# Score groups of three steps in six PSUM banks, one bank for the other work, in a cross-attention kernel

## The chip, the cores and the metric

One NeuronCore of a Trainium2 chip runs the whole program. The metric is device time in microseconds (us) of one execution. The kernel before takes 739.46 us, the median of three executions (738.22 to 741.74).

## The reference

Eight batch elements; 256 queries and 1601 context positions each, width 256, 16 heads of 16.

```python
x = layer_norm(hidden, ln1_w, ln1_b)
q = (x @ q_w + q_b)                       # 8 x 256 x 256, 16 heads of 16
k = (ctx @ k_w + k_b); v = (ctx @ v_w + v_b)     # 8 x 1601 x 256
scores = einsum('bhqd,bhkd->bhqk', q, k) / 4     # masked
out = softmax(scores) @ v                 # 8 x 16 x 256 x 1601 probabilities
hidden = out @ cproj_w + cproj_b + hidden
y = layer_norm(hidden, ln2_w, ln2_b)
return hidden + gelu(y @ fc_w + fc_b) @ proj_w + proj_b      # inner width 1024
```

## The kernel before

The kernel is written engine by engine: each engine has its own instruction list in program order, and semaphores join the lists. Nothing is reordered by a scheduler. What stands ahead of an instruction in its engine's list holds it up.

The work of a batch is cut into 4 slots of 4 heads, and a slot into 13 steps (KT) of 128 context positions; a batch has 52 steps. In a step TensorE (PE) forms the scores of 4 heads (4 matmuls of 64 rows, two at a time, L1140), ScalarE (ACT) takes the exponential of all 1024 columns in one instruction (L596) and writes it to a buffer of `pr`, and PE multiplies it by V (the "value products", L1147, 8 matmul instructions per step, in four column tiles of 32) into the bank `O`.

Between the steps PE does "units", nearly all for the next batch: 8 K units (`k_unit`, a K tile of 384 or 450 columns as a product of three terms), 13 V units (`v_unit`, one tile of 128 positions), the turning of the normalised x (XT), the Q product, the output projection of the batch before (`cproj`), and 8 maxima (`max_unit`, scores of a sample of the keys, from which VectorE takes each query's largest value). VectorE (DVE) empties the bank of every unit. K and Q go to DRAM and come back in the layout of the scores: `store_k`, then `first_fill` (7 DMAs a slot, issued by SP), which a slot's first maximum waits for. The maxima go into rows of `qst` by `first_rows` and are due when the slot's scores begin.

The eight PSUM banks are: `S` 4 banks (two steps of scores), `O` one bank of value products, `KB` (K units and half of the maxima), `MB` (the other half), `XB` (V, XT, Q, output projection).

Two steps make a pair; a batch has 26. PE's list for pair p is: the scores of both steps, each behind a wait for the exponential two steps earlier; the units that the tables `K_AT`, `V_AT`, `MAX_AT` and the rest put at p; the value products of the pair before. Where a slot ends inside a pair (p = 7 and 20) the units stand between its two steps of value products. DVE's list follows the same tables. GpSimd (POOL) splits the context of the batch after next into a high and a low part (L528, L533) as soon as the units that read the old one are done. In the last batch it splits the weights of the closing layers instead (L557 to L561). After the last batch the two layers of the MLP run (`mlp`).

Of the kernel before, what the change touches and what calls it, by code (L numbers as in the profile page):

```python
# [31 lines left out]
F32 = mybir.dt.float32  # L32
# [4 lines left out]
ALU = mybir.AluOpType  # L37
# [22 lines left out]
NKM = max(NKE)  # L60
CHUNK = [c for c in range(CH) for _ in range(NT[c])]
# [38 lines left out]
HEAD_MAX = [(s, j) for s in range(2) for j in range(NJ)]  # L100

# [5 lines left out]
def kb_pairs(b):  # L107

    return sorted([p for p in K_AT if b + 1 < B] + [p for p, (d, _, _) in MAX_AT.items() if b + d < B])


def mb_pairs(b):

    return sorted(p for p, (d, _, _) in MAX_AT.items() if b + d < B)


def xb_pairs(b):

    return sorted(([CPROJ_AT] if b > 0 else []) + ([XT_AT, Q_AT] + list(V_AT) if b + 1 < B else []))


def uses_before(head, pairs, b, p):

    return head + sum(len(pairs(i)) for i in range(b)) + sum(q < p for q in pairs(b))


KB_HEAD = len(HEAD_K) + len(HEAD_MAX)
MB_HEAD = len(HEAD_MAX)
XB_HEAD = KT + 2


def kb_use(b, p):
    return uses_before(KB_HEAD, kb_pairs, b, p)


def mb_use(b, p):
    return uses_before(MB_HEAD, mb_pairs, b, p)


def xb_use(b, p):  # L140
    return uses_before(XB_HEAD, xb_pairs, b, p)


def pair_of(table, what):
    return [p for p, w in table.items() if w == what][0]


XB_END = XB_HEAD + sum(len(xb_pairs(b)) for b in range(B))
MB_END = MB_HEAD + sum(len(mb_pairs(b)) for b in range(B))
KB_END = KB_HEAD + sum(len(kb_pairs(b)) for b in range(B))  # L150
# [1226 lines left out]
```

## Time and profile before

| | us |
|---|---|
| median of 3 executions (lowest, highest) | 739.46 (738.22, 741.74) |
| the profiled execution, its own time | 738.16 |
| its span, first to last instruction | 736.4 |
| PE busy with matmuls | 690.8 (94%) |
| ACT busy | 446.9 (61%) |
| DVE busy | 379.8 (52%) |
| POOL busy | 123.0 (17%) |

The span has four stretches: the head up to the first scores at 56.0 us, seven batches with units for the next one, a last batch without them (574.5 to 632.7 us) and the MLP. The granted clock is 0.991 of full speed on average, and 1.00 in all the batches. In the page's second part a PE digit of 9 says only that a matmul was in flight nine tenths of the time; how full PE is has to be read from the distance between the starts of its blocks.

### The profile page before, as it was taken

How to read it: one execution, taken by the hardware profiler on the slowest of the kernel's cores; microseconds unless marked ns; L12 is line 12 of the kernel's file. 1: busy time of each engine (PE TensorE's matmuls, PEld its weight loads, DVE VectorE, ACT ScalarE, POOL GpSimd, SP SyncE). 2: the span in 40 equal slices, each digit the busy share in tenths (PEclk: the TensorE clock that was granted, in tenths of full speed). 3: DMA queues.
4: the chain of work that ended last, by engine and by line, in shares of the span. 5: the costliest groups of instructions: out<-in, count | busy, mean ns of one | idle time of the engine just before them, and what ended most of it. 6: DMA issues, size and time to landing. Idle time of an engine off the chain costs nothing.

```text
span 736.4 us, 16791 instructions
## 1 busy us (share of the span) xinstructions
PE 690.8 (94%) x7026; PEld 471.3 (64%) x7026; DVE 379.8 (52%) x848; ACT 446.9 (61%) x471; POOL 123.0 (17%) x90
## 2 busy tenths in 40 slices
PE   2579999999999999999999999999999988999997
PEld 2566665666566656665666566656665544697897
DVE  5755654554355435543555345534653372467663
ACT  5406668656865686668666765676567888622320
POOL 6222041003200320032002300230000071011010
PEclk9889999999999999999999999999999999999999
DMA  9678565446534653564456445645442700000001
GB/s 307 196 252 296 187 208 199 145 155 214 202 133 169 212 192 136 177 213 170 158 176 213 154 174 175 214 143 185 151 174 92 281 3 1 1 29 8 22 30 32
DMA packets 51082, 113.77 MB, mean 155 GB/s; under 512 B 6858, under 2 KB 39986, under 8 KB 49722
## 3 DMA queue, kind: packets, MB, share of 16 engines
q1 hardware_dynamic: 40488, 80.56, 32.5%
q10 hardware_dynamic: 10514, 32.08, 11.9%
q8 instruction: 58, 0.95, 0.5%
q14 instruction: 22, 0.18, 0.1%
HBM read 65.30 MB, written 47.06 MB: 153 GB/s over the span
## 4 chain that ended last, share of the span: by engine, by line
PE 77%; ACT 12%; DVE 5%; issue 2%; DMA 2%; ACTq 1%; DVEq 0%
PE O L1147 22%; PE S L1140 16%; ACT pr L596 12%; PE O L1077 11%; PE XB L1077 10%; PE O L1234 6%; PE S L1077 5%; PE XB L1114 2%; PE XB L1174 2%; PE MB L1127 2%; DMA k_scr<-kpart 1%; DVE kpart L741 1%; DVE kpart L744 1%; DVE g_lo L911 1%; DMA cols_s<-in_cols 1%
## 5 line engine op out<-in xcount | busy, mean ns | idle before, releaser
L596 ACT ACTIVATE pr<-S 128x1024 f32<-128x1024 f32 x416 | 400.5, 1024 | 204.2 <-PE S L1140 171.9
L1147 PE MATMUL O<-pr,vsl 128*17 128x256 f32 x3328 | 223.1, 382 | 1.3 <-DVE ot L806 1.3
L1140 PEld LDWEIGHTS S<-qst,kst 64*128 64x128 f32 x1664 | 115.0, 185 | 111.3 <-ACT pr L596 75.6
L1140 PE MATMUL S<-qst,kst 64*128 64x256 f32 x1664 | 169.6, 311 | 11.6 <-ACT pr L596 7.7
L1147 PEld LDWEIGHTS O<-pr,vsl 128*17 128x17 f32 x3328 | 74.7, 96 | 77.2 <-issue 14.9
L741 DVE TENSOR_SCALAR kpart<-O,cols_s 128x384 fp32r<-128x384 f32 x64 | 40.6, 634 | 117.2 <-PE O L1077 117.2
L528 POOL CAST c_hi<-cT 128x768 fp32r<-128x768 f32 (+1 forms) x28 | 23.9, 852 | 323.0 <-DMA cT<-in_ctx_t 170.4
L787 DVE TENSOR_REDUCE mx<-MB 128x2 fp32r<-128x512 f32 x64 | 44.1, 689 | 51.4 <-PE MB L1127 51.3
L1077 PE MATMUL O<-c_hi,w_hi 128*128 128x384 f32 (+1 forms) x128 | 52.3, 409 | 19.4 <-POOL c_lo L533 10.4
L755 DVE TENSOR_TENSOR vsl<-XB,rows_s 128x256 f32<-128x256 f32 (+1 forms) x104 | 43.3, 416 | 51.2 <-PE XB L1077 51.2
L1077 PE MATMUL XB<-w_hi,c_hi 128*128 128x256 f32 (+1 forms) x208 | 66.6, 320 | 2.9 <-DVE vsl L755 2.7
L533 POOL TENSOR_TENSOR c_lo<-cT,c_hi 128x768 fp32r<-128x768 f32 (+1 forms) x32 | 61.0, 1908 | 5.8 <-ACT c_hi L592 3.5
L1077 PE MATMUL XB<-w_lo,c_hi 128*128 128x256 f32 (+1 forms) x208 | 59.0, 284 | 0.0
L614 ACT ACTIVATE g<-S,cols_s 128x512 f32<-128x512 f32 x32 | 22.1, 690 | 60.6 <-PE S L1077 53.5
L1077 PE MATMUL XB<-w_hi,c_lo 128*128 128x256 f32 (+1 forms) x208 | 58.8, 283 | 0.0
L806 DVE STREAM_TRANSPOSE ot<-O 128x256 f32<-128x256 f32 x32 | 14.4, 450 | 73.1 <-PE O L1147 72.4
L1077 PEld LDWEIGHTS XB<-w_hi,c_hi 128*128 128x128 f32 (+1 forms) x208 | 39.0, 187 | 17.7 <-issue 8.2
L1077 PE MATMUL O<-c_lo,w_hi 128*128 128x384 f32 (+1 forms) x128 | 45.5, 355 | 0.0
L1077 PE MATMUL O<-c_hi,w_lo 128*128 128x384 f32 (+1 forms) x128 | 45.4, 355 | 0.0
L790 DVE TENSOR_REDUCE mx<-O 128x2 fp32r<-128x512 f32 x64 | 43.6, 681 | 0.0
L1077 PEld LDWEIGHTS O<-c_hi,w_hi 128*128 128x128 f32 x128 | 24.9, 194 | 28.6 <-issue 15.8
L744 DVE SCALAR_TENSOR_TENSOR kpart<-O,cols_s,kpart 128x384 fp32r<-128x384 f32 x64 | 40.6, 635 | 2.3
(96 smaller groups left out, 834.0 us busy)
## 6 DMA issues: line engine op xcount, KB each, us to landing
kst<-k_scr SPq DMA_DIRECT2D x89, 400.2 KB
k_scr<-kpart SPq DMA_DIRECT2D x48, 384.0 KB, 3.3
v_scr<-vsl ACTq DMA_DIRECT2D x8, 1768.0 KB, 6.0
cT<-in_ctx_t ACTq DMA_DIRECT2D x21, 384.0 KB, 4.7
k_scr<-kpart SPq DMA_DIRECT2D x16, 449.0 KB, 3.0
qst<-q_scr SPq DMA_DIRECT2D x87, 64.0 KB
q_scr<-qpart SPq DMA_DIRECT2D x16, 256.0 KB, 2.5
cT<-in_ctx_t ACTq DMA_DIRECT2D x7, 449.0 KB, 3.5
```

Source lines behind the costliest of these rows:

```text
L528: nc.gpsimd.tensor_copy(c_hi[:, c, :, 0:n], cT[:, c, :, 0:n]).then_inc(hi_done, 1)
L533: nc.gpsimd.tensor_tensor(c_lo[:, c, :, 0:n], cT[:, c, :, 0:n], c_hi[:, c, :, 0:n].bitcast(F32), ALU.subtract).then_inc(lo_done, 1)
L596: nc.scalar.activation(pr[:, n % PBUF, :], S[:, 2 * (n % 2):2 * (n % 2) + 2, :] .rearrange("p a n -> p (a n)"), ACT.Exp).then_inc(s_.exp_d ...
L741: nc.vector.tensor_scalar(kpart[:, i, 0, 0:n], KB[:, 0:n], bk_s[:, mt:mt + 1], None, ALU.add).then_inc(kh_done, 1)
L744: nc.vector.scalar_tensor_tensor(out=kpart[:, i, 1, 0:n], in0=KB[:, 0:n], scalar=bk_s[:, mt:mt + 1], in1=kpart[:, i, 0, 0:n].bitcast(F32), ...
L755: nc.vector.tensor_tensor(vsl[0:m, b % 2, :, kt, :].rearrange("p s (h w) -> p s h w", w=VW)[:, :, :, 0:HD], XB[0:m, 0:D].rearrange("p (s h ...
L787: nc.vector.tensor_reduce(mx[:, s % 2, :, j], MB[:, :].rearrange("p (q k) -> p q k", q=QT), AX.X, ALU.max, negate=True).then_inc(mb_taken, 1)
L790: nc.vector.tensor_reduce(mx[:, s % 2, :, NJ + j], KB.rearrange("p (q k) -> p q k", q=QT), AX.X, ALU.max, negate=True).then_inc(kb_taken, 1)
L1077: last = nc.tensor.matmul(dst, a, c, start=i == 0, stop=i == len(terms) - 1)
L1140: last = nc.tensor.matmul(S[:, 2 * (n % 2) + g_, j * LQ:(j + 1) * LQ], kst[rows_, s, j, kt * P:(kt + 1) * P], qst[rows_, s, j, :], start=T ...
L1147: last = nc.tensor.matmul(O[32 * h:32 * h + VW, 0, 0:LQ], vsl[:, par, s, kt, h * VW:(h + 1) * VW], pr[:, n % PBUF, h * LQ:(h + 1) * LQ], s ...
L1234: last = nc.tensor.matmul(O[:, n % 2, 0:D], w[:, i, cut], v[:, i, :], start=i == 0 and m == 0, stop=i == NI - 1 and m == 2)
```

## The change

- `S` has six banks in three places, `S[:, 2i:2i+2]`. A slot's 13 steps form five groups of 3, 2, 3, 2 and 3 (`BOUNDS`); a batch has 20 groups (`GROUPS`) in place of 26 pairs. `pr` has six buffers, three for each of two groups.
- The maxima have no bank of their own: they take the third score place, which a group of two steps leaves free, and DVE empties both banks with one instruction. The group that follows can use the third place once DVE has done so (`emptied`).
- All other units use one bank `U`, in turn. V is made two tiles at a time: 7 units in place of 13.
- The units are put anew on the 20 groups; the last K unit of the first half (`(0, 3)`) moves from pair 6 (steps 12, 13) to group 7 (steps 18 to 20).
- On DVE, `divide` comes ahead of the maximum of its group; the inverse root of the second norm in the last batch (`inverse_root`, 11 small instructions) moves from pair 12 to group 7. The load of the MLP's weights in the last batch moves from step 4 to step 6, each V tensor's store from step 48 of the batch before to step 10 of its own.
- In the head the K units alternate between `U` and a bank of `S`, the last maximum comes after the last V unit, and the first scores wait for all of them to be emptied.

```diff
+DEEP = 3
+PBUF = 2 * DEEP
+BOUNDS = [0, 3, 5, 8, 10, KT]
+SLOTG = len(BOUNDS) - 1
+GROUPS = SLOTS * SLOTG
-K_AT = {0: (0, 0), 2: (0, 1), 4: (0, 2), 6: (0, 3), 8: (1, 0), 10: (1, 1), 12: (1, 2), 14: (1, 3)}
+K_AT = {0: (0, 0), 1: (0, 1), 5: (0, 2), 7: (0, 3), 9: (1, 0), 10: (1, 1), 12: (1, 2), 14: (1, 3)}
+V_AT = {6: 0, 8: 1, 11: 2, 15: 3, 16: 4, 17: 5, 19: 6}
+CPROJ_AT, XT_AT, Q_AT = 2, 3, 4
+def max_of(b, g):
+
+    s, k = divmod(g, SLOTG)
+    b_, s_ = b + (s + 2) // SLOTS, (s + 2) % SLOTS
+    return (b_, s_, k // 2) if len(steps_of(g)) < DEEP and b_ < B else None
...
-        S = stack.enter_context(nc.psum_tensor("S", [P, 4, 512], F32))
-        O = stack.enter_context(nc.psum_tensor("O", [P, 2, 512], F32))
-        MB = stack.enter_context(nc.psum_tensor("MB", [P, 512], F32))
-        XB = stack.enter_context(nc.psum_tensor("XB", [P, 512], F32))
-        KB = O[:, 1, :]
+        S = stack.enter_context(nc.psum_tensor("S", [P, 2 * DEEP, 512], F32))
+        O = stack.enter_context(nc.psum_tensor("O", [P, 512], F32))
+        U = stack.enter_context(nc.psum_tensor("U", [P, 512], F32))
+        SUMS, XB, MB = O[:, 0:LQ], S[:, 4, :], S[:, 5, :]
...
+                nc.vector.tensor_reduce(mx[:, s % 2, :, j:HG:NJ].rearrange("p q g -> p g q"),
+                                        S[:, 2 * i:2 * i + 2, :].rearrange("p g (q k) -> p g q k", q=QT), AX.X, ALU.max,
+                                        negate=True).then_inc(peak_taken, 1)
...
+            def v_pair(b, i):
+                bank_free(u_taken, v_use(b, 2 * i))
+                for t, kt in enumerate(tiles_of(i)):
+                    last = v_products(b, kt, U[:, t * D:(t + 1) * D])
+                last.then_inc(u_ready, 1)
...
+            def emptied(b, g, i):
+
+                for at in range(GROUPS * b + g - 1, -1, -1):
+                    b_, g_ = divmod(at, GROUPS)
+                    if i < len(steps_of(g_)):
+                        return pe.wait_ge(first.exp_done, STEPS * b_ + steps_of(g_)[i] + 1)
+                    if max_of(b_, g_):
+                        return pe.wait_ge(peak_taken, max_use(b_, g_) + 1)
...
             for b in range(B):
-                for p in range(PAIRS):
-                    for n in (2 * p, 2 * p + 1):
-                        scores(b, n)
...
+                for at in range(GROUPS):
+                    scores(b, at)
+                    if max_of(b, at):
+                        emptied(b, at, DEEP - 1)
+                        max_unit(*max_of(b, at), DEEP - 1)
+                    units(b, at)
+                    if at > 0:
+                        for n in steps_of(at - 1):
+                            values(b, n)
```

PE's list in the middle of a batch, steps 36 to 41 before (`S<-qst,kst` are scores, 4 a step; `O<-pr,vsl` value products, 4 a step here, where the profile counts 8; `XB<-` a V unit):

```order
L1147 MATMUL O<-pr,vsl 17x256 x8
L1140 MATMUL S<-qst,kst 128x256 x8
L1147 MATMUL O<-pr,vsl 17x256 x8
L1140 MATMUL S<-qst,kst 128x256 x8
L1147 MATMUL O<-pr,vsl 17x256 x4
L1077 MATMUL XB<-w_hi,c_hi 128x256
...
L1077 MATMUL XB<-w_hi,c_lo 128x256
L1147 MATMUL O<-pr,vsl 17x256 x4
```

The same engine after the change, the group of steps 39 to 41, with two V tiles, and the group of two steps behind it, with a maximum:

```order
L1179 MATMUL S<-qst,kst 128x256 x12
L1106 MATMUL U<-w_hi,c_hi 128x256
...
L1106 MATMUL U<-w_hi,c_lo 128x256
L1186 MATMUL O<-pr,vsl 17x256 x12
L1179 MATMUL S<-qst,kst 128x256 x8
L1167 MATMUL S<-kst,qst 128x256 x4
```

Blocks of one kind have grown by half, and the value products of a pair that spans two slots are no longer split around a unit. The rows left out are four products of the one V tile before and ten of the two tiles after.

DVE's list in the last batch, before (`mx<-` maxima, `mrow` their turning, `rs` the inverse root with its first and last row here, `ot`, `rec`, `good`, `att` the division of a slot):

```order
L824 SCALAR_TENSOR_TENSOR good<-ot,good 128x8
L828 TENSOR_TENSOR att<-ot,rec 128x8x16
L787 TENSOR_REDUCE mx<-MB 128x2
L790 TENSOR_REDUCE mx<-O 128x2
L787 TENSOR_REDUCE mx<-MB 128x2
L790 TENSOR_REDUCE mx<-O 128x2
L801 STREAM_TRANSPOSE mrow<-mx 128x2x32
L702 TENSOR_SCALAR rs<-rs 128x14
...
L714 SCALAR_TENSOR_TENSOR rs<-rs 128x14
```

and after:

```order
L859 SCALAR_TENSOR_TENSOR good<-ot,good 128x8
L863 TENSOR_TENSOR att<-ot,rec 128x8x16
L825 TENSOR_REDUCE mx<-S 128x2x2
L729 TENSOR_SCALAR rs<-rs 128x14
...
L741 SCALAR_TENSOR_TENSOR rs<-rs 128x14
L825 TENSOR_REDUCE mx<-S 128x2x2
L836 STREAM_TRANSPOSE mrow<-mx 128x2x32
```

The eleven instructions of the inverse root stood behind the batch's last maximum and now stand ahead of it.

## Rows read from the trace of the kernel before

**Rows 1.** Busy time by stretch: batch 0, a middle batch, the last batch
```profile
core 0: us, PE busy (x) PEld busy (x) DVE busy (x) ACT busy (x) POOL busy (x), PEclk, DMA share, GB/s
56.00:128.40 72.40, 70.79 (x779) 45.73 (x778) 40.96 (x110) 49.49 (x52) 15.35 (x11) 1.00 0.63 224
277.00:351.30 74.30, 73.37 (x808) 47.52 (x804) 35.85 (x78) 50.19 (x53) 12.40 (x9) 1.00 0.51 177
574.50:632.70 58.20, 52.33 (x668) 27.95 (x664) 23.19 (x62) 50.89 (x55) 15.35 (x5) 1.00 0.17 63
```
**Rows 2.** Timeline of PE: start, us, line, tiles; two pairs of a middle batch
```profile
319.47 0.74 PE L1140 MATMUL S<-qst,kst 64*128 64x256 f32 x8
320.14 0.39 PE L1077 MATMUL XB<-w_hi,c_hi 128*128 128x256 f32 x1
...
321.04 1.06 PE L1147 MATMUL O<-pr,vsl 128*17 128x256 f32 x16
322.03 0.74 PE L1140 MATMUL S<-qst,kst 64*128 64x256 f32 x8
322.70 0.47 PE L1077 MATMUL O<-c_hi,w_hi 128*128 128x450 f32 x1
...
324.12 1.06 PE L1147 MATMUL O<-pr,vsl 128*17 128x256 f32 x16
```
**Rows 3.** Timeline of PE around step 41 of that batch
```profile
337.28 0.50 PE L1140 MATMUL S<-qst,kst 64*128 64x256 f32 x4
338.16 0.50 PE L1140 MATMUL S<-qst,kst 64*128 64x256 f32 x4 [0.38 <-ACT pr L596]
338.60 0.63 PE L1147 MATMUL O<-pr,vsl 128*17 128x256 f32 x8
339.15 0.39 PE L1077 MATMUL XB<-w_hi,c_hi 128*128 128x256 f32 x1
```
**Rows 4.** Waits of that batch: engine, for whom, us in total, times, longest
```profile
PEld S L1140 <- ACT pr L596: 8.9, 22, 0.6
```
**Rows 5.** DVE emptying banks, from the groups by line
```profile
L787 DVE TENSOR_REDUCE mx<-MB 128x2 fp32r<-128x512 f32 x64 | 44.1, 689 | 51.4 <-PE MB L1127 51.3
L744 DVE SCALAR_TENSOR_TENSOR kpart<-O,cols_s,kpart 128x384 fp32r<-128x384 f32 x64 | 40.6, 635 | 2.3
```
**Rows 6.** Timeline of SP: a K store, slot 0 filled; and PE's maximum
```profile
301.39 0.37 SPq L403 DMA_DIRECT2D k_scr<-kpart  x1
304.16 1.89 SPq L350 DMA_DIRECT2D kst<-k_scr  x3
308.01 0.58 SPq L364 DMA_DIRECT2D kst<-mask_scr  x1
...
325.86 0.36 PE L1127 MATMUL MB<-kst,qst 63*128 63x256 f32 x1
```
**Rows 7.** DMA issues: size, median us to landing
```profile
pj_raw<-in_pj ACTq DMA_DIRECT2D x1, 1024.0 KB, 11.0
```
**Rows 8.** Timeline of DVE, POOL and ACT's queue in the last batch
```profile
578.16 0.45 ACTq L634 DMA_DIRECT2D pj_raw<-in_pj  x1
589.21 1.90 POOL L557 CAST fc_hi<-fc_raw 128x2048 fp32r<-128x2048 f32 x1 [80.29 <-DMA pj_raw<-in_pj]
593.02 4.57 POOL L560 TENSOR_TENSOR fc_lo<-fc_raw,fc_hi 128x2048 fp32r<-128x2048 f32 x1
593.11 4.51 DVE L824 SCALAR_TENSOR_TENSOR good<-ot,good 128x8 f32<-128x8 f32 x1
597.53 4.72 POOL L561 TENSOR_TENSOR pj_lo<-pj_raw,pj_hi 128x2048 fp32r<-128x2048 f32 x1
...
602.75 0.13 DVE L702 TENSOR_SCALAR rs<-rs 128x14 int32<-128x14 int32 x1
```
**Rows 9.** Timeline of PE, first scores, and of ACT, first exponentials
```profile
56.04 0.74 PE L1140 MATMUL S<-qst,kst 64*128 64x256 f32 x8
58.10 3.77 ACT L596 ACTIVATE pr<-S 128x1024 f32<-128x1024 f32 x4 [31.14 <-issue]
```

More of the change, by code:

```diff
@@ L100 @@
 HEAD_MAX = [(s, j) for s in range(2) for j in range(NJ)]
+HEAD_X = ["v0", "v1", "v2", "xt", "q"] + [f"v{t}" for t in range(3, KT)]
 class Section:
     pass
[L107 to L124, printed above, removed]
@@ L127 @@
[L127 to L150, printed above, removed]
@@ L155, in k_use, with u_groups, u_use, max_use @@
+def u_groups(b):
+    return sorted(([CPROJ_AT] if b > 0 else []) + ([XT_AT, Q_AT] + list(K_AT) + list(V_AT) if b + 1 < B else []))
+def u_use(b, g):
+    return len(HEAD_K) + sum(len(u_groups(i)) for i in range(b)) + sum(q < g for q in u_groups(b))
+def max_use(b, g):
+    return len(HEAD_MAX) + sum(max_of(*divmod(i, GROUPS)) is not None for i in range(GROUPS * b + g))
+def group_of(table, what):
+    return [g for g, w in table.items() if w == what][0]
+U_END = u_use(B, 0)
 def k_use(b, mt, c):
-    return HEAD_K.index((mt, c)) if b == 0 else kb_use(b - 1, pair_of(K_AT, (mt, c)))
+    return HEAD_K.index((mt, c)) if b == 0 else u_use(b - 1, group_of(K_AT, (mt, c)))
@@ new lines, in v_pair_evac, with xt_evac @@
+            def v_pair_evac(b, i):
+                dve.wait_ge(pads_set, 10)
+                if i == 0 and b >= 2:
+                    dve.wait_ge(v_out, 16 * (b - 1))
+                dve.wait_ge(u_ready, v_use(b, 2 * i) + 1)
+                for t, kt in enumerate(tiles_of(i)):
+                    last = v_tile(b, kt, U[:, t * D:(t + 1) * D])
+                last.then_inc(u_taken, 1)
+            def xt_evac(b, use):
+                bank, ready, taken = x_bank(b)
+                dve.wait_ge(ready, use + 1)
@@ L1112, in q_unit @@
+            def q_unit(b, use):
+                bank, ready, taken = x_bank(b)
+                bank_free(taken, use)
                 for mt in range(2):
                     for k in range(KC):
-                        last = nc.tensor.matmul(XB[:, mt * LQ:(mt + 1) * LQ], w_qc_s[:, 0, k, mt * P:(mt + 1) * P],
+                        last = nc.tensor.matmul(bank[:, mt * LQ:(mt + 1) * LQ], w_qc_s[:, 0, k, mt * P:(mt + 1) * P],
                                                 xT[:, k, :], start=k == 0, stop=k == KC - 1)
-                last.then_inc(xb_ready, 1)
@@ L1301, in _ @@
-            values(B - 1, STEPS - 2)
+                if g in K_AT and more:
+                    k_unit(b + 1, *K_AT[g])
+                if g == CPROJ_AT and b > 0:
+                    cproj(b - 1, u_use(b, g))
+                if g == XT_AT and more:
+                    xt_unit(b + 1, u_use(b, g))
+                if g == Q_AT and more:
+                    q_unit(b + 1, u_use(b, g))
+                if g in V_AT and more:
+                    v_pair(b + 1, V_AT[g])
+                if b == B - 1 and g == YT_AT:
+                    pe.wait_ge(u_taken, u_use(b, g))
+                    turn_y(first, 0, [0])
```

447 lines of the change are left out of this document (219 added, 228 removed).

## The prediction

> **What bounds the kernel now.** I read the busy time by stretch first, then PE's timeline inside a middle batch, then the waits, then the other engines at the places that the change touches.
>
> The stretches [rows 1] show a middle batch of 74.3 us in which PE has a matmul in flight for 73.4 and ACT is busy for 50.2, DVE for 35.9, POOL for 12.4. The six batches from 128.4 to 574.5 us are alike: 446.1 in all. In the last batch PE is at 52.3 and ACT at 50.9 of 58.2: both are near the end there. The clock was 1.00 in all of them. So PE's list is the sum to make, and what counts is the distance from one block's start to the next.
>
> From the timeline [rows 2], with each block followed by one of another kind: scores of two steps take 0.67 (319.47 to 320.14), a V unit 0.90, value products of two steps 0.99, a K unit of 450 columns 1.42. Two slopes come out of these. K and V units are both six products, and 6 x 450 columns take 0.52 more than 6 x 256: 0.447 ns a column, so a K unit of 384 columns takes 1.24 and a second V tile in the same block 0.69 (estimates). A single step of value products, 338.60 to 339.15 [rows 3], takes 0.55, where two take 0.99: 0.44 a step and 0.11 for the block. A step of scores is four matmuls of 256 columns, two at a time: 512 columns, 0.23, so 0.21 for the block. That is the point: of a block's time a part is paid once per block, however long it is.
>
> PE also waits for ACT. The scores of a pair can't start before the exponential of two steps earlier; where a pair has no unit, PE comes too soon. In [rows 3] the scores that began at 337.28 need 1.31 in place of 0.67. The waits of the batch [rows 4] count 8.9 us in 22 cases, but most of each (0.4) is the turn from value products to scores, which is there without any wait too (it is inside the 0.99). What lengthens score blocks beyond 0.67 is six cases of 0.24 to 0.64 in a batch, 2.5 us in all; the one shown is the longest.
>
> **The change, a middle batch.** 26 pairs become 20 groups, 12 of three steps and 8 of two.
> - Scores: 26 x 0.67 = 17.4 before; 12 x 0.90 + 8 x 0.67 = 16.2 after. Minus 1.2.
> - Value products: 26 x 0.99 and two blocks more for the two split pairs (0.11 each) = 26.0; after 12 x 1.43 + 8 x 0.99 = 25.1. Minus 0.9.
> - V: 13 x 0.90 = 11.7; after six blocks of 1.59 and one of 0.90 = 10.4. Three V units stood right behind a K unit, where a block costs less; I take 0.3 off for that. Minus 1.0.
> - Waits for ACT: minus 2.5, since each group of three now has a unit. Group by group, a group of three takes 0.90 + 1.24 + 0.99 = 3.1 or more on PE, and ACT, whose four exponentials take 3.77 [rows 9], needs 2.8. The two groups without a unit are groups of two with a maximum: 0.67 + 0.4 + 1.43 = 2.5 against 1.9. Only at the batch's first group is ACT behind by a little: plus 0.3.
> - Maxima, K, Q, XT and the projection keep their number and length: nothing.
>
> Sum: 1.2 + 0.9 + 1.0 + 2.2 = 5.3 us, 74.35 to about 69.0; six batches: 31.8.
>
> What could replace the wait? The single bank `U` must be empty before the next unit. Between one group's unit and the next stand value products (0.99 at least) and scores (0.67 plus a maximum of about 0.4, or 0.90): 1.9 to 2.3. Emptying a K bank takes DVE two instructions of 0.635 [rows 5], 1.3 with the start. It is covered, unless DVE is still busy with the maximum ahead of it. A maximum of both banks is 1024 columns in one instruction; 512 take 0.689 [rows 5], so between 0.69 and 1.38, and I take 1.25. It is ready 1.24 before the K unit is, so the K bank's emptying starts on time or 0.2 late. Covered by 0.3 or more. Without that cover a batch would pay some 0.5 at each of seven places. The third score place is asked for again after a unit, value products and two steps of scores, 3 us after the maximum: covered too, as long as DVE isn't held up.
>
> DMA: the last K unit of the first half moves to group 7, and the first maximum that needs slot 0 stands in group 11. Between them PE has 0.99, group 8 (0.67 + 0.4 + 1.59 + 1.43), group 9 (0.90 + 1.24 + 0.99), group 10 (0.90 + 1.24 + 1.43) and 0.67 of scores: 12.4 us. Before, the store of K was issued at 301.39 and the seventh DMA of the fill had been issued at 308.59 [rows 6]: 7.2, to which come 1.7 from the unit's end to the store (two DVE instructions and their starts) and the landing of the last DMAs. The landing isn't shown; I bound it by nothing and by the 2.8 that the K store took before the fill could start. So 8.9 to 11.7, and I take 10.6. Before, PE came for it at 325.86, 24 us after the store. The slack falls to about 1.8 us, and I count no loss.
>
> **Head and batch 0.** The batch saves the same 5.3. PE had scores at 56.04, but ACT's first exponential came at 58.10, after its own DMA issues [rows 9]. Now PE's scores wait until the last maximum is emptied, some 1.8 later, with no K and V unit done in the meantime; the K units of the head, in two banks, win part of that back. Together minus 4.0 (minus 1 to minus 6).
>
> **The last batch.** It has no units, and ACT sets it: 52 exponentials at 0.94 are 49, with two more ACT instructions for the turned y and a few short waits 53.7 rather than 58.2. But the inverse root now stands ahead of the maximum of group 8. The weights' load is issued two steps later than before, so about 5.5 us into the batch; it lands 11.0 later [rows 7], and POOL splits them from 17 to 30 us of the batch, as it did from 589.21 to 602.25 [rows 8]. In that stretch DVE's tiny `good` (128x8) took 4.51 us, the whole length of POOL's subtraction, and the inverse root came at 602.75 only, past it. Now DVE reaches it at about 20. If its small instructions are held as that one was, they get through one by one at the seams of POOL's work and end at about 32; the maximum behind them is taken at 33.5, and PE can't write the third step of group 9, due at 25.4. That is 8 us of PE, some 7 of ACT: 60.7. If they are held only once (to 25.5), 56.0. I take 60.0: plus 1.8.
>
> The Trainium skill has a rule for this (SBUF — State Buffer, section "SBUF: two separate sides"): a DVE instruction with two SBUF inputs or in a two-port mode and a GpSimd instruction exclude each other for the whole length of whichever began first. The row of 4.51 us agrees. Nine of the eleven instructions of the inverse root have two SBUF inputs, so by the rule the loss of 7 us is due, by a reading of the row as a single accident the batch takes 53.7.
>
> The MLP keeps its list; only the names of its banks change: nothing.
>
> **Sum.** 738.16 (own time of the profiled execution, 1.8 over its span) - 31.8 - 4.0 + 1.8 = 704.2. The median of the runs is 1.3 above that execution, so 705.5.
>
> **Rivals.**
> - The last batch isn't held (the load lands later or earlier, or DVE's small instructions slip through). Against it: the row of 4.51, and a stretch of 13 us that is hard to miss. The batch takes 53.7: 699.
> - Small waits take the place of the one removed: DVE late with bank `U` or the third place (0.5 at seven places a batch, 3.5), or slot 0 landing 1 to 3 us after PE comes for it. For it: the slack there falls from over 10 us to 1.8, and loads of the context share the DMA queues. Over seven batches 7 to 21 us: 712 to 726, middle 717.
> - The fill of slot 0 comes so late that it costs more than the change gives. The place is the first maximum of group 11, PE's list stands behind it, and the price is the full lateness, seven times. It decides from 34/7 = 4.9 us of lateness on, that is, 17.3 us from K unit to landing, where I have 10.6; a store of K behind other transfers of the queue could add 2, a context load in the same microseconds 2 more. At 7 us: 754.
> - The change does not do what it says, since PE's fixed part per block is not per block but per change of tile: then only the 2.2 of waits and some of the V term come, 3 a batch: 721. Against it: the 0.55 and 0.99 in neighbouring blocks of one kind.
>
> **Chances.** Forecast 0.45, last batch not held 0.2, small waits 0.2, late fill over the gain 0.05, fixed part not saved 0.1. The time is that of the forecast, 705.5. Its own range is 701 to 710; with the rivals' 699 and most of 712 to 721 the range is 697 to 720. A difference of 0.5% (3.7 us) is about what this measurement can tell from none. Faster by more 0.91, within it 0.04, slower 0.05.
>
> **What would show it.** In the profile of the changed kernel: batches 1 to 6 at 69 us each, with three-step scores at 0.90 and three-step value products at 1.43; V pairs at 1.6; PE's waits for ACT nearly gone in them; the maximum of both banks at 1.25 on DVE; no wait of PE for a DMA at group 11; in the last batch one wait of PE of 7 to 8 us behind DVE's inverse root, with DVE's small instructions stretched to POOL's 4.6 us. The prediction is wrong if a middle batch takes over 71 us, or if PE waits there for `U` or for the fill.

## The result, and the profile after

| us | before | after |
|---|---|---|
| median (lowest, highest) | 738.84 (738.2, 741.74), 4 executions | 720.61 (716.67, 725.14), 4 executions |
| the profiled execution, own time | 738.16 | 719.08 |
| its span, mean granted clock | 736.4, 0.991 | 717.3, 0.968 |

The ratio is 0.9744, with a 95% interval from 0.9714 to 0.9774: faster by 2.6%. The forecast was 705.5 with a range of 697 to 720. The median lies just over the range's upper end, the profiled execution (719.08) just inside it. The direction was right, and nearly half of the expected gain (34.0) isn't there: it is 19.1 between the two profiled executions.

Busy time by stretch in the changed kernel: batch 0, a middle batch, batch 6, the last batch, the MLP. The first three kinds answer to [rows 1].

```profile
core 0: us, PE busy (x) PEld busy (x) DVE busy (x) ACT busy (x) POOL busy (x), PEclk, DMA share, GB/s
59.10:131.90 72.80, 69.53 (x770) 48.05 (x770) 39.10 (x97) 49.03 (x52) 10.99 (x9) 0.94 0.53 181
271.30:341.10 69.80, 68.98 (x806) 46.82 (x802) 35.41 (x70) 49.69 (x53) 12.27 (x10) 1.00 0.54 189
...
480.90:549.60 68.70, 68.70 (x808) 46.71 (x804) 35.19 (x70) 49.69 (x53) 3.51 (x3) 1.00 0.48 168
549.60:613.90 64.30, 53.51 (x676) 29.83 (x672) 25.16 (x58) 50.68 (x55) 15.18 (x5) 0.92 0.24 85
613.90:717.30 103.40, 96.92 (x622) 86.08 (x618) 64.34 (x136) 27.32 (x40) 7.18 (x3) 0.99 0.07 22
```

Read three things. The middle batch went from 74.3 to 69.8, and batch 6, which loads no context for a later batch, to 68.7 with PE in flight all the time. The last batch went up, from 58.2 to 64.3, with PE and ACT as busy as before (53.5 and 50.7): 10.8 of it is PE idle. And the clock column is below 1.00 in batch 0 and in the last batch, where it had been 1.00.

By the starts of each batch's first scores, the difference of the two profiled executions is:

| stretch | forecast | measured |
|---|---|---|
| head and batch 0 (up to 128.44; now 131.91) | -4.0 | +3.5 |
| batches 1 to 6 (446.0; now 417.7) | -31.8 | -28.4 |
| last batch (58.3; now 64.4) | +1.8 | +6.1 |
| MLP (103.7; now 103.4) | 0 | -0.3 |
| sum | -34.0 | -19.1 |

**The blocks.** PE's timeline in the middle batch, the place that answers to [rows 2] and [rows 3] (in the K unit, rows between its first and last product are left out):

```profile
307.22 0.98 PE L1179 MATMUL S<-qst,kst 64*128 64x256 f32 x12
308.13 0.44 PE L1106 MATMUL U<-c_hi,w_hi 128*128 128x384 f32 x1
...
309.39 1.49 PE L1186 MATMUL O<-pr,vsl 128*17 128x256 f32 x24
310.81 0.74 PE L1179 MATMUL S<-qst,kst 64*128 64x256 f32 x8
312.36 0.51 PE L1167 MATMUL S<-kst,qst 63*128 63x256 f32 x4 [0.81 <-DMA kst<-mask_scr]
312.80 0.39 PE L1106 MATMUL U<-w_hi,c_hi 128*128 128x256 f32 x1
...
314.42 0.84 PE L1186 MATMUL O<-pr,vsl 128*17 128x256 f32 x12
```

From start to start: three-step scores 0.91 (forecast 0.90), K 1.26 (1.24), three-step value products 1.42 (1.43), a pair of V tiles 1.62 (1.59). One block is off: the two-step scores at 310.81 take 1.55 in place of 0.57, because what follows them, group 11's maximum, waits for the last DMA that fills slot 0. This is the wait on which the forecast had 1.8 us of slack.

The waits in this batch, engine by engine (us in total, times, longest), answer to [rows 4]:

```profile
PEld S L1179 <- ACT pr L618: 2.7, 7, 0.4
...
PEld S L1167 <- issue: 1.0, 1, 1.0
...
PE S L1167 <- DMA kst<-mask_scr: 0.8, 1, 0.8
```

PE's weight loads waited for ACT 22 times before and 7 times now. The wait for the fill shows up twice here, as 0.8 of PE and as 1.0 of "issue" on the weight load: it is one wait, and the list alone would put a part of it down to nothing. The distance between blocks doesn't have that fault: by it the maximum of group 11 comes 0.8 to 1.1 late in batches 1 to 5, 2.8 in batch 0 and not at all in batch 6.

**The fill.** SP's and ACT's queues at that place answer to [rows 6]:

```profile
303.52 1.91 SPq L370 DMA_DIRECT2D kst<-k_scr  x3
305.48 2.07 SPq L378 DMA_DIRECT2D qst<-q_scr  x3
307.59 0.58 SPq L384 DMA_DIRECT2D kst<-mask_scr  x1
```

```profile
304.61 0.37 ACTq L363 DMA_DIRECT2D cT<-in_ctx_t  x1
...
308.01 0.37 ACTq L363 DMA_DIRECT2D cT<-in_ctx_t  x1
```

The K unit (0, 3) ended on PE at 299.13 and the maximum was due at 311.39: 12.3 us, as forecast (12.4). The issue of the fill's last DMA ended at 308.17, and PE could start at 312.36 only: 4.2 for the landing, where I had allowed at most 2.8. In the same microseconds two loads of context (384 KB each) were under way, issued by ACT at 304.61 and 308.01; in the trace they land 7.3 and 5.0 us later. From 303 to 315 us the fill's queue took 61.7% of the time of the 16 DMA engines and the loads' queue 19.9%.

In batch 0 something else is late as well. There 4.8 us pass from the issue of the K store (88.30) to the first issue of the fill (93.13), where batch 3 has 2.8 (300.75 to 303.52), so the fill is issued 2 us late; the first load of context is issued at 92.18 only, when it is already 1 us late. The K store itself lands 4.7 us after its issue in place of 2.6, and a transfer of the instruction queue (89.17 to 90.85) ran in the middle of it.

**The last batch.** DVE and POOL, answering to [rows 8]:

```profile
568.86 1.21 DVE L825 TENSOR_REDUCE mx<-S 128x4 fp32r<-128x1024 f32 x1
569.99 3.40 DVE L729 TENSOR_SCALAR rs<-rs 128x14 int32<-128x14 int32 x1
573.42 4.47 DVE L731 TENSOR_SCALAR rs<-rs 128x14 int32<-128x14 int32 x1
577.92 0.17 DVE L736 SCALAR_TENSOR_TENSOR rs<-rs 128x14 f32<-128x14 f32 x1
...
579.80 1.23 DVE L825 TENSOR_REDUCE mx<-S 128x4 fp32r<-128x1024 f32 x1
```

```profile
568.79 4.56 POOL L581 TENSOR_TENSOR fc_lo<-fc_raw,fc_hi 128x2048 fp32r<-128x2048 f32 x1
573.31 4.55 POOL L582 TENSOR_TENSOR pj_lo<-pj_raw,pj_hi 128x2048 fp32r<-128x2048 f32 x1
```

The inverse root's first two instructions work on 14 numbers a partition. The first ends with POOL's first subtraction (573.39 and 573.35), the second with POOL's second (577.89 and 577.86). The other nine take 0.17 each once POOL is done. The maximum, which reads PSUM, ran for its usual 1.2 while POOL was at work. PE, same stretch and a later one:

```profile
574.45 0.74 PE L1179 MATMUL S<-qst,kst 64*128 64x256 f32 x8
581.08 0.80 PE L1179 MATMUL S<-qst,kst 64*128 64x256 f32 x4 [5.89 <-DVE mx L825]
581.80 1.91 PE L1186 MATMUL O<-pr,vsl 128*17 128x256 f32 x16
...
596.86 1.01 PE L1179 MATMUL S<-qst,kst 64*128 64x256 f32 x12
600.07 1.12 PE L1242 MATMUL U<-idn,fc_raw 128*128 128x128 f32 x4 [2.20 <-ACT pj_raw L631]
601.11 2.60 PE L1186 MATMUL O<-pr,vsl 128*17 128x256 f32 x24
```

Group 9's scores start at 574.45, but their third step has to wait for the maximum that stands behind the root: 7.36 from this block to the next in place of 0.91, a loss of 6.5 (forecast 8). The second wait was not in the forecast. The normalised y is turned in two halves, both in bank `U` now; the second half can't be written before ACT has copied the first, and ACT's copy stands behind the last exponential of its group. Before, the halves had a bank each, and PE has no such wait in the last batch.

**The head.** PE up to the first scores, answering to [rows 9] (products within a unit and other units are left out):

```profile
38.11 0.28 PE L1106 MATMUL S<-w_hi,c_hi 128*128 128x256 f32 x1
...
45.47 0.80 PE L1167 MATMUL S<-kst,qst 63*128 63x256 f32 x4 [6.85 <-DMA kst<-mask_scr]
46.19 0.58 PE L1106 MATMUL S<-w_hi,c_hi 128*128 128x256 f32 x1
...
56.73 0.80 PE L1167 MATMUL S<-kst,qst 63*128 63x256 f32 x4
59.08 1.65 PE L1179 MATMUL S<-qst,kst 64*128 64x256 f32 x12 [1.55 <-issue]
```

The last K unit of the head began at 34.35, where it had begun at 42.52. That won nothing: slot 0's fill landed at about 45.5 (before, PE's first maximum stood at 47.09), and PE sat idle for 6.85. In the seven variants below that add no matmuls the first maximum starts between 45.4 and 46.4 too, behind idle stretches of 2.4 to 7.5 us. From 40.2 to 64.1 the granted clock was half (1.2 GHz in place of 2.4; in this part the kernel before had it from 33.8 to 40.6), and the same products have rows of 0.58 and 0.42 where they have 0.39 and 0.28 elsewhere.

### The profile page after: what moved, and what is told of

It is laid out like the page before. It is cut to its first block, busy times and chain, and to the rows that moved or that the text cites. A ratio compares the mean times of both kernels' runs of the same rounds, so it can differ in the third digit from the quotient of the medians.

```text
span 717.3 us, 16705 instructions
## 1 busy us (share of the span) xinstructions
PE 668.1 (93%) x7026; PEld 474.4 (66%) x7026; DVE 375.9 (52%) x784; ACT 443.2 (62%) x471; POOL 122.5 (17%) x90
## 4 chain that ended last, share of the span: by engine, by line
PE 78%; DMA 6%; ACT 6%; DVE 4%; SPq 3%; issue 1%; ACTq 0%; DVEq 0%
PE O L1186 24%; PE U L1106 19%; PE S L1179 16%; PE S L1106 6%; ACT pr L618 4%; PE U L1285 3%; PE O L1285 3%; DMA kst<-mask_scr 3%; PE S L1167 3%; PE U L1226 2%; PE U L1156 2%; ACT kst L674 1%; DMA cT<-in_ctx_t 1%; DMA k_scr<-kpart 1%; SPq L378 1%
## 5 line engine op out<-in xcount | busy, mean ns | idle before, releaser
L768 DVE TENSOR_SCALAR kpart<-U,cols_s 128x384 fp32r<-128x384 f32 (+1 forms) x60 | 37.9, 631 | 114.5 <-PE U L1106 114.4
L825 DVE TENSOR_REDUCE mx<-S 128x4 fp32r<-128x1024 f32 x64 | 78.0, 1219 | 32.8 <-PE S L1167 32.5
L777 DVE TENSOR_TENSOR vsl<-U,rows_s 128x256 f32<-128x256 f32 (+1 forms) x91 | 34.7, 419 | 52.7 <-PE U L1106 52.3
L641 ACT ACTIVATE g<-S,cols_s 128x512 f32<-128x512 f32 x32 | 22.1, 689 | 60.6 <-PE S L1106 53.4
L1106 PE MATMUL U<-c_hi,w_hi 128*128 128x384 f32 (+1 forms) x120 | 48.7, 406 | 10.2 <-POOL c_lo L554 10.1
L1106 PE MATMUL U<-w_hi,c_hi 128*128 128x256 f32 (+1 forms) x182 | 56.5, 310 | 0.0
L1106 PE MATMUL U<-w_lo,c_hi 128*128 128x256 f32 (+1 forms) x182 | 51.7, 284 | 0.0
L1106 PE MATMUL U<-w_hi,c_lo 128*128 128x256 f32 (+1 forms) x182 | 51.6, 284 | 0.0
L1106 PE MATMUL U<-c_hi,w_lo 128*128 128x384 f32 (+1 forms) x120 | 42.9, 357 | 0.0
L1106 PE MATMUL U<-c_lo,w_hi 128*128 128x384 f32 (+1 forms) x120 | 42.6, 355 | 0.0
L1167 PE MATMUL S<-kst,qst 63*128 63x256 f32 x256 | 28.9, 304 | 14.6 <-DMA kst<-mask_scr 10.9
L771 DVE SCALAR_TENSOR_TENSOR kpart<-U,cols_s,kpart 128x384 fp32r<-128x384 f32 (+1 forms) x60 | 38.0, 633 | 2.1
L841 DVE STREAM_TRANSPOSE ot<-O 128x256 f32<-128x256 f32 x32 | 14.4, 449 | 45.5 <-PE O L1186 45.4
```

The lines of the kernel that those rows point to most:

```text
L768: nc.vector.tensor_scalar(kpart[:, i, 0, 0:n], k_room(b, use)[:, 0:n], bk_s[:, mt:mt + 1], None, ALU.add).then_inc(kh_done, 1)
L771: nc.vector.scalar_tensor_tensor(out=kpart[:, i, 1, 0:n], in0=k_room(b, use)[:, 0:n], scalar=bk_s[:, mt:mt + 1], in1=kpart[:, i, 0, 0:n].b ...
L777: return nc.vector.tensor_tensor(vsl[0:m, b % 2, :, kt, :].rearrange("p s (h w) -> p s h w", w=VW)[:, :, :, 0:HD], bank[0:m, :].rearrange( ...
L825: nc.vector.tensor_reduce(mx[:, s % 2, :, j:HG:NJ].rearrange("p q g -> p g q"), S[:, 2 * i:2 * i + 2, :].rearrange("p g (q k) -> p g q k", ...
L1106: last = nc.tensor.matmul(dst, a, c, start=i == 0, stop=i == len(terms) - 1)
L1167: last = nc.tensor.matmul(S[:, 2 * i + g_, q * SAMPLE:(q + 1) * SAMPLE], query_set(rows_, s, j, q), kst[rows_, s, j, q * SAMPLE:(q + 1) * ...
```

## The experiments

All ratios are to the kernel before on the same chip; where there is one execution only, its own time stands. Kernels e5 to e7 contain e3's edit.

### e3_k_earlier: more room for the fill

```diff
-K_AT = {0: (0, 0), 1: (0, 1), 5: (0, 2), 7: (0, 3), ...
+K_AT = {0: (0, 0), 1: (0, 1), 5: (0, 2), 6: (0, 3), ...
-V_AT = {6: 0, 8: 1, ...
+V_AT = {7: 0, 8: 1, ...
```

> The changed kernel with the last K unit of the first half at group 6 and the first V pair at group 7 (they change places). In batches 1 to 5 the scores before group 11's maximum took 1.55 us in place of 0.58 and the wait ends with the mask's DMA, the last of slot 0's fill. K comes some 3.7 us earlier, so if the fill is late because K is: that wait is gone, batches 1 to 5 take 68.8 us in place of 69.8, batch 0 loses its 2.8 us of wait and the half clock behind it (together 4 or so), total minus 8 to 9. Rival, the fill is late because of something else in the queues: the wait stays.

Measured: 706.59 (704.69 to 709.53), ratio 0.9535 (0.9509 to 0.9561), where the changed kernel has 0.9744 (0.9714 to 0.9774). Batches 1 to 6 take 68.71 to 68.73 each. The middle batch of its profile, and PE at group 11:

```profile
264.08:332.80 68.72, 68.72 (x806) 46.68 (x802) 35.21 (x70) 49.70 (x53) 12.34 (x10) 1.00 0.56 192
```

```profile
303.59 0.74 PE L1179 MATMUL S<-qst,kst 64*128 64x256 f32 x8
304.16 0.40 PE L1167 MATMUL S<-kst,qst 63*128 63x256 f32 x4
```

The block of scores ahead of the maximum is back at 0.57, and PE has no gap in the whole batch. One group earlier (16.2 us from the unit's end to the maximum instead of 12.3) removes the wait in all seven batches. Six middle batches give 5.4 us back, batch 0 4.5 (72.83 to 68.31: there the wait had been 2.6, with a half clock behind it from 101.6 to 105.1), and the last batch 2.8 (64.35 to 61.59), which this edit doesn't touch. In all that is 12.5 us between the two profiled executions, where 8 to 9 were expected, and the last part isn't the edit's doing: the wait behind the root is 5.4 in place of 5.9, and the wait for the turned y is 2.2 as before, but no half clock follows it here. From that wait's start to ACT's second copy 5.7 us pass in place of 7.2.

### e4_ctx_later: the same wait from the side of the traffic

```diff
-CTX_AT = [24, 28, 32, 36]
+CTX_AT = [31, 34, 37, 40]
```

> The changed kernel with the four context loads of a batch at steps 31, 34, 37 and 40 in place of 24, 28, 32 and 36. In batch 6, which loads no context, PE did not wait at group 11 (68.7 us against 69.8). If the first load, issued while slot 0 is being filled, is what makes the fill late: the wait at group 11 (0.97 us in each of batches 1 to 5) falls to 0 to 0.2 and these batches take 68.8. Rival, batch 6 differs for another reason: 69.8 as before.

Measured: 710.81 (one execution). The K unit stays where the change put it; only the steps at which ACT issues the loads of context are later. Periods of batches 0 to 6: 69.66, 68.71, 68.73, 69.68, 68.73, 68.71, 68.73. PE's waits for the fill, in the whole execution, changed kernel first and this one second:

```profile
PE S L1167 <- DMA kst<-mask_scr: 10.9, 4, 6.9
```

```profile
PE S L1167 <- DMA kst<-mask_scr: 4.1, 3, 2.4
```

The first row's longest, and 2.4 of the second, stand in the head. The list puts the wait of some middle batches down to ACT, so the periods are the measure. By them the wait is gone in five of seven batches without moving a K unit. So the fill can be short enough for the forecast's 12.4 us, and what makes it 1 us late in batches 1 to 5 is the context's loads beside it; batch 6 of the changed kernel, which has no such loads and no wait, says the same.

Batches 0 and 3 keep 1.2 and 0.9 us of the wait with no load in the way. In both the fill was issued late: 4.6 and 4.1 us after the K store in place of 2.8. Of the 35 fills of slot 0 in batches 0 to 6 of the five kernels in which this K unit keeps its place (the changed one, e1, e2, e4, e9), eight were issued 4.0 to 5.0 us after the store and the others 2.8 to 3.1. In each of the eight a transfer of the instruction queue ran between the two; the same is so in only six of the other 27. That this transfer is the cause is likely and not shown: no run changes it.

### e1_root_late: the inverse root behind POOL's work

```diff
-                if b == B - 1 and g == 7:
+                if b == B - 1 and g == 10:
```

> The changed kernel with DVE's inverse root of the last batch moved from group 7 to group 10, behind the maximum of group 8; nothing else. In the changed kernel the scores of group 9 took 7.36 us (574.45 to 581.80) while DVE's rs instructions stood 3.40 and 4.47 us behind POOL's subtractions. If that is what PE waited for: these scores take 0.9 to 1.6, the granted clock does not fall behind them, and the last batch takes 57 to 58 in place of 64.35 us, the whole 6.5 to 7 less. Rival, the DVE stall only uncovers another wait (the maximum of group 6, or the division, is held by the same POOL work): the batch still takes over 61.

Measured: 713.01 (712.68 to 714.34), ratio 0.9622 (0.9605 to 0.9638). The last batch takes 56.52 in place of 64.35 (57 to 58 expected). DVE's same two instructions there:

```profile
583.11 0.13 DVE L729 TENSOR_SCALAR rs<-rs 128x14 int32<-128x14 int32 x1
583.28 0.18 DVE L731 TENSOR_SCALAR rs<-rs 128x14 int32<-128x14 int32 x1
```

0.13 and 0.18 in place of 3.40 and 4.47, with the same operands, once POOL is done: what they cost is POOL's work, not theirs. The scores of group 9 take 0.91, and the half clock from 579.5 to 586.3 is gone with the wait; the one behind the turned y stays (596.6 to 600.0).

### e2_turn_early: ACT's copy of the turned y ahead of its group's exponentials

```diff
-                    if b == B - 1 and n == steps_of(YT_AT + 1)[-1]:
+                    if b == B - 1 and n == steps_of(YT_AT + 1)[0]:
...
-                    if b == B - 1 and n == steps_of(YT_AT + 2)[-1]:
+                    if b == B - 1 and n == steps_of(YT_AT + 2)[0]:
```

> The changed kernel with ACT's two halves of the turned y taken before the first exponential of groups 15 and 16 (steps 39 and 42) and not before the last (41 and 43). In the changed kernel PE stood 2.2 us before the second half of the turn (600.07) and ACT then idled 3.26 us (to 604.19). Theory, the one bank U makes PE wait for ACT's place in its list: scores of group 15 near 1.2 and not 3.21, ACT's gap under 1, the last batch 2.5 to 3.5 us shorter than 64.35. Rival, ACT has to catch up anyway: no more than 1 us shorter.

Measured: 722.45 (one execution), so as a whole no better. In the place that it touches it does what it should:

```profile
603.72 1.01 PE L1179 MATMUL S<-qst,kst 64*128 64x256 f32 x12
604.88 0.66 PE L1242 MATMUL U<-idn,fc_raw 128*128 128x128 f32 x4 [0.15 <-ACT pj_raw L631]
```

The scores ahead of the second half take 1.16 in place of 3.21, no half clock follows, and the last batch takes 58.97 in place of 64.35. That is 5.4 where 2.5 to 3.5 were expected. Of it 2.1 is the wait; 1.2 is a shorter wait behind the root (4.7 for 5.9; POOL's work began 1.3 earlier in the batch), which isn't the edit's; the rest is the half clock, which e3 lacks at this place with the wait still there. The rest of the execution took it back: in this one PE waited for the fill for 20.4 us in 7 cases, 7.4 of them in the head (10.9 in 4 in the changed kernel's, 6.9 in the head), and batches 2, 3 and 5 took 71.3, 71.3 and 73.0. The edit doesn't touch the fill; how late it comes differs from one execution to the next.

### e5_head_places: each score place waits for its own maximum only

```diff
             def emptied(b, g, i):
...
-                pe.wait_ge(peak_taken, len(HEAD_MAX))
+                if i < 2:
+                    return pe.wait_ge(peak_taken, len(HEAD_MAX) - 1 + i)
                 pe.wait_ge(u_taken, len(HEAD_K))
```

> The kernel e3 (changed kernel, last K unit of the first half one group earlier) with the first scores waiting, place by place, only for what is in their own place: step 0 for the third maximum, step 1 for the fourth, step 2 for all V and K units. In e3 the last maximum (56.29) takes 2.06 us to the first scores, 1.3 of it DVE's emptying. Theory, that wait is on PE's path: the first scores start 1.0 to 1.4 us sooner after the last maximum, but step 1 must still wait, so the batch after them gains 0.2 to 0.6. Rival, ACT or PE is free to use it in full: 1.2 us sooner at batch 1.

Measured: 705.76 (one execution; e3's are 704.69 to 709.53). The first scores start at 56.47 in place of 58.35, but batch 1 at 126.12 in place of 126.66: of 1.9 us at the front 0.5 is left a batch later. The first block lasts 2.71 in place of 1.58, since its second step still has to wait for DVE to take the last maximum (1.2 in the waits), so that the K unit behind it starts 0.8 earlier only.

### e6_head_busy and e9_busy_alone: PE kept at work through the wait

```diff
             v_unit(7)
+            pe.wait_ge(u_taken, len(HEAD_K))
+            for i in range(56):
+                nc.tensor.matmul(U[:, 0:D], w_hi[:, 0, 0, 0:P], w_hi[:, 0, 1, :], start=True, stop=True)
             max_unit(0, 0, 0, 0)
```

e6 has this on top of e3, e9 on the changed kernel alone. For e6:

> The kernel e3 with 56 extra matmuls of 256 columns into the free bank U while PE waits in the head for slot 0 to land (38 to 45 us); they compute nothing that is used. In the changed kernel the granted clock was at half from 40.2 to 64.1 us, behind an idle stretch of PE of 6.85 us, and V units took 1.28 to 1.58, scores of three steps 1.58. If the idle stretch is what lowers the clock: full clock from about 45 us on, the four maxima and six V units from the first maximum to the first scores take 9 to 10.5 us in place of 12.7, three-step scores 0.9, batch 1 starts 3 to 5 us earlier. Rival, the chain there is set by DVE emptying the one bank and the clock hardly counts: under 1.5 us earlier.

For e9:

> The changed kernel with nothing else but 56 more matmuls of 256 columns on the U bank while TensorE waits for the first maximum of batch 0 (their result isn't read). In the changed kernel TensorE stands idle from 38.5 to 45.47, its granted clock is half from 40.2 to 64.1, and batch 1 begins at 131.91 (before: 128.44). Theory: that half clock is a part of the 3.5 us by which the head and batch 0 came out longer. With the gap filled the clock stays whole up to the first scores (three-step scores of 0.9 in place of 1.58, K of 1.26 in place of 2.22), and batch 1 begins 1.0 to 2.0 us earlier, at 129.9 to 130.9; the rest of the 3.5 is the wait of 2.6 us before group 11's maximum in batch 0 and stays; time 718 to 720 as against 720.6. Rival: in the head everything waits for transfers and evictions anyway and the clock takes nothing: batch 1 begins at 131.4 to 132.4 and the time is unchanged at 720 to 721. Second rival: the clock is the whole of it, and batch 1 begins by 128.5 to 129.5.

Measured, e6: 704.93 (one execution); batch 1 starts at 125.56 (e3: 126.66), 1.1 earlier where 3 to 5 were expected, and so within what the rival gave. Both halves of the expectation can be seen in it: from the first maximum to the first scores it takes 10.0 us in place of 12.7, as expected, but the 56 matmuls last beyond the landing of slot 0, and the first maximum starts at 48.21 in place of 45.64.

Measured, e9: 720.25 (718.66 to 724.18), ratio 0.9748 (0.9716 to 0.9780); batch 1 starts at 126.62, where the changed kernel has 131.91. Busy time by stretch of 10 us, the changed kernel and then e9:

```profile
40.00:50.00 10.00, 4.53 (x20) 3.71 (x20) 2.94 (x4) 0.00 (x0) 1.96 (x2) 0.51 0.96 341
50.00:60.00 10.00, 7.27 (x35) 5.80 (x36) 4.58 (x8) 0.08 (x1) 3.67 (x3) 0.50 0.52 183
```

```profile
40.00:50.00 10.00, 8.81 (x70) 7.95 (x69) 3.09 (x5) 0.00 (x0) 2.14 (x2) 1.00 0.95 337
50.00:60.00 10.00, 6.82 (x43) 5.74 (x44) 4.03 (x7) 2.45 (x3) 3.55 (x3) 0.86 0.59 193
```

With PE at work in the gap the clock is whole from 40 to 57 us. The first scores come 2.1 earlier (59.08 to 56.94) and batch 0 is 3.1 shorter, nearly all of it at group 11, where the wait for the fill is 1.2 in place of 2.8 and no half clock follows. So the profile gained 5.3 us by batch 1, more than even the rival that laid everything on the clock had given (2.4 to 3.4): I had the second part, the fill in batch 0, down as fixed. Whether the matmuls bring it isn't shown: the fill of batch 0 was issued 2.8 us after the K store here and 4.8 in the changed kernel, and e9's batch 4 has the 4.8. But the time of e9 is not faster than the changed kernel's. Its profiled execution lost most of the gain again at two fills (batches 4 and 5 took 72.85 and 70.87). This kernel can't show what a gain in the head is worth while the fills are on the edge; e10 below can.

### e7_split: is the fixed part paid per block?

Batches 2 and 4 only: where a group has three steps, one step of value products stands ahead of the unit and two behind it, as the kernel before had it at two places. Nine blocks more in a batch, the same products.

```diff
+                    back = [(b, n) for n in steps_of(at - 1)] if at > 0 else [(b - 1, n) for n in steps_of(GROUPS - 1)]
+                    early = 1 if b in (2, 4) and at > 0 and len(back) == DEEP else 0
+                    for of_batch, n in back[:early]:
+                        values(of_batch, n)
                     units(b, at)
...
+                    for of_batch, n in back[early:]:
+                        values(of_batch, n)
```

> The kernel e3 with, in batches 2 and 4 alone, the value products of three steps cut in two where a unit follows (one step ahead of the unit, two behind it; nine places a batch). Theory, a fixed part per block (0.11 for value products, 0.13 to 0.14 counted with the unit beside it): batches 2 and 4 take 1.0 to 1.3 us more than batches 1, 3 and 5 (68.7). Rival, the fixed part is paid only between scores and value products: no difference. If bank U isn't emptied in time any more: over 2 us more, with waits before units.

Measured: batches 1, 3 and 5 take 68.71, batches 2 and 4 69.75 (whole time 710.75, one execution). A split place and the two batches beside each other:

```profile
201.70 0.63 PE L1186 MATMUL O<-pr,vsl 128*17 128x256 f32 x8
202.26 0.44 PE L1106 MATMUL U<-c_hi,w_hi 128*128 128x384 f32 x1
...
203.50 1.06 PE L1186 MATMUL O<-pr,vsl 128*17 128x256 f32 x16
```

```profile
196.97:266.73 69.76, 69.76 (x807) 45.73 (x804) 35.20 (x70) 49.70 (x53) 12.34 (x10) 1.00 0.56 189
266.73:335.43 68.70, 68.70 (x806) 46.68 (x802) 35.22 (x70) 49.68 (x53) 12.33 (x10) 1.00 0.56 192
```

1.04 us for nine blocks (1.0 to 1.3 expected), 0.116 each: 0.56 and 0.99 in place of 1.42. The 0.11 a block of value products that the forecast read from two neighbouring rows is right to 0.01, and the rival by which it isn't paid per block is out. The 0.21 of a block of scores has no such run.

### e8_all and e10_all_busy: the edits together

e8 has e1, e2, e3 and e5; e10 has e6's matmuls as well.

> e1, e2, e3 and e5 together. If the losses are separate: batches at 68.7, the last batch at 54 to 56, the head as in e5. From e3's 706.6: minus 7.8 (e1) minus 0.5 to 2 (what e2 gives once the root is out of the way) minus 0.5: 697 to 699. Rival, they share a cause in the last batch: no better than 700.

> The kernel with the root late, the turned y early, the last K unit a group earlier and the freed score places (698.3 us, batch 1 beginning at 127.70 with a half clock from 40.2 to 64.1 in its profiled run), with the same 56 matmuls in the head. Theory (the idle stretch of 9 us before the first maximum brings the half clock, and the half clock costs time in batch 0): batch 1 begins at 125.3 to 126.3, as in the kernel with the last K unit a group earlier and these matmuls (125.56), and the time is 696 to 697.3. Rival (the clock costs nothing that transfers don't take anyway): batch 1 begins at 127.2 to 128 and the time is 698 to 699.

Measured, e8: 698.3 (695.03 to 702.04), ratio 0.9435 (0.9403 to 0.9466), within the 697 to 699 expected. Measured, e10: 695.49 (693.62 to 696.0), ratio 0.939 (0.937 to 0.9411). Both beat both kernels; the intervals of the two overlap a little (0.9403 to 0.9411), so that e10 is faster than e8 is likely and not settled by the times alone. By the profiles batch 1 starts at 127.70 in e8 and at 124.85 in e10, 2.9 apart, as the medians are (2.8); I had expected 1.4 to 2.4. A middle batch and the last batch of e10:

```profile
124.90:193.60 68.70, 68.70 (x807) 46.69 (x804) 35.91 (x73) 49.68 (x53) 12.36 (x10) 1.00 0.56 192
537.20:590.50 53.30, 49.96 (x675) 28.33 (x672) 17.19 (x58) 50.12 (x55) 15.19 (x5) 1.00 0.29 102
```

The last batch takes 53.4 in both. The kernels that differ in it give a table of two by two (the changed kernel, e2, e1, and e8 or e10, each from its one profile):

| last batch, us | y's copy as in the change | y's copy early |
|---|---|---|
| root at group 7 | 64.35 | 58.97 |
| root at group 10 | 56.52 | 53.36 |

By the table the root costs 7.8 or 5.6, the copy 5.4 or 3.2, both together 11.0. These are good to some 3 us only: the seven kernels whose last batch is that of the first cell (the changed one, e9, and e3 to e7) read 61.5 to 64.6 there, with the four that have no half clock behind the turned y (e3, e5, e6, e7) at 61.5 to 62.7. From those, which share e3's edit with e8 and e10, both together are 8.2 to 9.4. That the last cell is the one without either wait is firm, and the forecast's value for a last batch that isn't held was 53.7.

## Why the prediction was right in its direction and half right in its size

- **Middle batches, -5.3 each: right as a sum of blocks.** Block for block the lengths are within 0.03, and with the fill's wait taken away (e3) a batch takes 68.7, where 69.0 was forecast. e7 shows that the fixed part per block of value products is real. Where this term gave less than forecast (-28.4 for -31.8) that is the next point.
- **The fill of slot 0, "I count no loss": the step that failed in the middle batches.** What was available came out right (12.3 for 12.4). What was needed was put at 8.9 to 11.7 and took 13.2, 299.13 to 312.36. The mis-sized piece is the landing of the last DMAs, 4.2 for at most 2.8. My upper bound was taken from a K store that had the queues nearly to itself, while the rows of the context's loads, which the second rival names, stood in the same microseconds. That rival said 1 to 3 us late; it was 0.8 to 1.1 in five batches, 2.8 in batch 0 and nothing in batch 6. In batch 0 the landing of the K store is late too, 4.7 for 2.6. The rival had 0.2 of the chances and 717 in the middle; it is the case that came true, beside the others.
- **Head and batch 0, -4.0: the sign was wrong.** "The K units of the head, in two banks, win part of that back" failed: they are done 8 us earlier and win nothing, since the first maximum waits for the fill. I costed PE's work there without asking when its data land. The idle stretch that came of it was followed by 23.9 us at half clock, worth 2.1 up to the first scores (e9). The rest of the 7.5 is the wait in batch 0 with its own half clock (3.1 in e9, which still waits 1.2 there; 4.5 in e3, where the wait is gone), and 0.9 to 2.2 that no run isolates; the wait of the first scores for the last maximum, which I had put at 1.8, is the nearest candidate, and e5 shows that little of it (0.5) reaches batch 1.
- **Last batch, +1.8 for +6.1: right in its mechanism, and a second one missed.** The held root came in the place and in the way forecast: two long holds, the root done at 30.2 us of the batch (32 forecast), the maximum behind it at 31.5 (33.5), 6.5 of PE (8). The trace agrees with the Trainium skill's rule on the two elementwise engines (SBUF — State Buffer, section "SBUF: two separate sides"), by which one is held for the whole length of the other's instruction: the rows end together, 573.39 beside 573.35 and 577.89 beside 577.86, and e1, past POOL's work, has no such hold. I had counted the nine instructions with two SBUF inputs; those held were the two with one, since they came first. No run shows in which mode they ran, so that the rule covers them isn't shown. What I missed is the turned y: with a single bank `U` its second half waits for ACT. I had looked for what waits for `U` only in batches with units.
- **The clock.** I read 1.00 in all batches before and carried it over. In the changed kernel each new idle stretch of PE named above (6.85 in the head, 2.6 in batch 0, 5.9 and 2.2 in the last batch) was followed by a stretch at half clock, and each of these is gone in a kernel that takes its wait away (e10, e3, e1, e2). The waits were priced at their own length; their tails came on top. The short ones don't always have a tail: e3, e5, e6 and e7 keep the wait of 2.2 for the turned y and show no half clock behind it.
- **The MLP, 0:** -0.3.
- **Other rivals.** That the last batch isn't held: out here; e8, in which neither wait stands, takes 53.4, near the 53.7 of that rival. That the fill costs more than the gain: out; it was 1 us late, and once 2.8, where 4.9 in every batch would have been needed.
- **The number.** 720.6 comes from three misses in one direction: 3.4 in batches 1 to 6, 7.5 in the head and batch 0, 4.3 in the last batch. The range reached to 720 for the rival of small waits alone, whose price in the batches was only in part paid; that the other two misses fill it up so nearly is luck.

## What to carry to other kernels

When a block list is regrouped, the sum of its blocks can be forecast to some tenths of a us from neighbouring rows; what decides the rest is each wait whose slack is cut, and a transfer's landing has to be bounded with the other queues' transfers of the same microseconds in it, not from a row where the queues were quiet. When two banks become one, walk through every pair of writes to that bank in every stage, the last batch too. Work finished earlier on an engine is worth nothing until the trace says when its input lands, and here an idle TensorE was often charged twice: for the wait, and for the half clock after it. A profile of one execution can also flatter an edit in a place that it doesn't touch, as the last batch of e3 does.

## What was unexpected of the hardware

- The granted clock fell to half not only in the head but within batches that had run at 1.00, behind single waits: 3.4 us of half clock (101.6 to 105.1) behind 2.6 us of idle PE, 6.8 (579.5 to 586.3) with 5.9 of idle PE, 3.4 (600.0 to 603.4) behind 2.2. It didn't fall behind each. From the first scores to the MLP, over the changed kernel and all its variants, the eight idle stretches of 4.7 to 6.4 us were all followed by some 6.8 us at half clock; of the fifteen of 2.2 to 2.9 us nine were followed by 3.4 us of it and six by none. In the head it was 23.9 us, in which PE was in flight only 4.5 of the first 10.
- Matmuls whose result nobody reads seem to buy time: 56 of them took 6.88 us in an idle stretch of the head, and e10 is 2.8 us below e8 in the median, with intervals that overlap a little.
- A store of 449 KB, alone in its queue, landed 4.7 us after its issue with a transfer of the instruction queue in it, and 2.6 without.
- A one-input instruction of DVE on 14 numbers a partition takes 3.40 or 4.47 us beside a POOL subtraction with two inputs, and 0.13 or 0.18 without, while DVE's maximum of 1024 columns from PSUM ran in its usual 1.2 in the same stretch.
